# Expert weights prepared while stage A empties, own orders of work for its filling and emptying, and its loop written out

## The reference

```python
x = layernorm(x + attention(x, Wq, Wk, Wv, Wo, bo))   # 16 heads of 8
x = layernorm(x + retention(x, ctx, ctx))             # rotated q and k, decay mask, 16 heads of 8, no weights
x = layernorm(x + moe(x, gate, w1, w3, w2))           # 8 experts, inner 512, top 2 of 8 by gate
# moe: out = sum over the chosen e of p_e * ((silu(x @ w1[e]) * (x @ w3[e])) @ w2[e])
```

## Time and profile before

| what | value |
|---|---|
| median of the runs | 1058.34 us |
| profiled execution, its own time | 1065.84 us |
| its span | 1063.7 us |
| mean granted TensorE clock | 0.903 |
| TensorE busy | 856.2 us, 80% |
| VectorE busy | 800.6 us, 75% |
| GpSimd busy | 650.5 us, 61% |
| ScalarE busy | 621.2 us, 58% |
| stage A, to the first matmul of stage B | 0 to 675.2 us |
| stage B | 675 to about 1003 us |
| stage C | to 1063.7 us |

### The profile page before, as it was taken

One profiled execution on the slowest core, in us unless ns is written; L12 is line 12 of the kernel. 1 busy time (PEld: TensorE's weight loads), 2 busy tenths in 40 slices (PEclk: granted clock), 3 DMA queues, 4 the chain that ended last, 5 costly groups with the idle time before them and its releaser, 6 DMA issues.

```text
span 1063.7 us, 36375 instructions
## 1 busy us (share of the span) xinstructions
PE 856.2 (80%) x12164; PEld 640.8 (60%) x12165; DVE 800.6 (75%) x2219; ACT 621.2 (58%) x1416; POOL 650.5 (61%) x738
## 2 busy tenths in 40 slices
PE   1573969899999899898987871599999999999600
PEld 1352546666567566565655541488888888888600
DVE  3776779999789788797765653588887888777565
ACT  1032446677667666676566862466666666666445
POOL 0353756699989989899777546144444444444443
PEclk9685989999999999999889975799999999999855
DMA  6223211222212313222121101222122112122076
GB/s 231 61 52 83 55 36 39 51 62 53 68 47 62 72 40 71 49 51 61 32 53 50 35 29 61 63 62 57 56 60 59 58 57 58 56 60 57 33 254 220
DMA packets 145252, 72.10 MB, mean 68 GB/s; under 512 B 75024, under 2 KB 134544, under 8 KB 145136
## 3 DMA queue, kind: packets, MB, share of 16 engines
q1 hardware_dynamic: 124800, 40.56, 16.3%
q0 software_dynamic: 8640, 17.84, 5.0%
q10 hardware_dynamic: 11696, 12.08, 3.5%
HBM read 42.11 MB, written 28.34 MB: 66 GB/s over the span
## 4 chain that ended last, share of the span: by engine, by line
PE 36%; POOL 7%; issue 5%; DMA 3%; DVE 3%; ACT 2%; SPq 1%; another core or an unknown queue 0%; POOLq 0%; ACTq 0%; DVEq 0%
PE QKV L770 9%; PE ST L770 9%; PE XT L798 5%; PE SC L798 5%; POOL prod_ev L1550 4%; POOL routed_rows L1567 2%; DMA prod_ev<-token_halves 2%; PE ST L640 1%; ACT q L923 1%; PE YY L788 1%; PE ST L655 1%; PE TR L788 1%; PE YY L588 1%; POOL rs L1530 1%; DMA routed_rows<-xe,pos 1%
## 5 line engine op out<-in xcount | busy, mean ns | idle before, releaser
L1550 POOL TENSOR_TENSOR prod_ev<-e_sb,q_v 128x512 f32<-128x512 f32 x256 | 295.9, 1190 | 101.3 <-PE YY L588 61.6
L1599 POOL DMA_INDIRECT token_halves<-w_new,tok_i x142 | 137.9, 971 | 39.4 <-issue 33.6
L1567 POOL DMA_INDIRECT routed_rows<-xe,pos x128 | 131.4, 1026 | 30.4 <-issue 29.4
L1150 DVE TENSOR_TENSOR prod_qk<-q_v,QKV 128x2048 f32<-128x2048 f32 x64 | 145.4, 2274 | 0.0
L1036 ACT ACTIVATE prod_qk<-QKV,silu_scale 128x512 f32<-128x512 f32 x142 | 95.9, 687 | 61.5 <-PE QKV L770 60.0
L1452 DVE TENSOR_TENSOR prod_ev<-prod_qk,prod_ev 128x1024 f16<-128x1024 f32 x71 | 87.0, 1225 | 54.2 <-ACT prod_ev L1027 34.4
L770 PE MATMUL QKV<-k_t,w_hl 128*128 128x256 f16 x852 | 117.1, 274 | 0.1
L770 PE MATMUL ST<-k_t,w_hl 128*128 128x256 f16 x852 | 117.0, 274 | 0.1
L411 POOL TENSOR_TENSOR marks<-half_c 128x1 f32<-128x1 f32 x103 | 19.9, 193 | 151.1 <-DVE w_new L1468 150.9
L1478 DVE SCALAR_TENSOR_TENSOR prod_qk<-ST,hid_scale,prod_qk 128x512 f32<-128x512 f32 x142 | 102.4, 744 | 10.1 <-ACT prod_qk L1036 7.1
L923 ACT ACTIVATE q<-XT,tab 128x256 f32<-128x256 f32 x256 | 96.6, 497 | 0.0
(11 more groups left out here) (169 smaller groups left out, 1791.9 us busy)
## 6 DMA issues: line engine op xcount, KB each, us to landing
w_new<-routed_rows SPq DMA_DIRECT2D x71, 130.0 KB
prod_ev<-token_halves SPq DMA_DIRECT2D x16, 512.0 KB, 5.0
x_sb<-x SPq DMA_DIRECT2D x32, 128.0 KB, 2.6
x_res<-x SPq DMA_DIRECT2D x128, 32.0 KB
head_rows<-o_n SPq DMA_DIRECT2D x32, 128.0 KB
o_t<-head_rows SPq DMA_DIRECT2D x64, 64.0 KB
ctx_sb<-ctx SPq DMA_DIRECT2D x32, 128.0 KB
out<-prod_qk ACTq DMA_DIRECT2D x16, 256.0 KB, 4.4
```

Source lines behind the costliest of these rows:

```text
L1150: eng.tensor_tensor(prod_qk[:, u, :, :].rearrange("p d (i j) -> p d i j", j=NH), q.unsqueeze(3).to_broadcast([P, HD, NH, NH]), k.unsqueeze ...
L1550: ins = eng.tensor_tensor(prod_ev[:, u, q, :, :, 0:HD], e_sb[:, it.slot(2), u, 64 * q:64 * q + 64].rearrange("p (i j) -> p j i", j=4).unsq ...
L1567: eng.indirect_dma_start(out=xs, out_offset=bass.IndirectOffsetOnAxis(ap=pos[:, r, 2 * u + k:2 * u + k + 1], axis=0), in_=xe[:, r, u, k, : ...
L1599: eng.indirect_dma_start(out=halves, out_offset=bass.IndirectOffsetOnAxis(ap=tok_i[:, s, u:u + 1], axis=0), in_=yw[:, s, u, :], in_offset= ...
```

## The change

1. **Weights.** Their preparation leaves the filling. w1 is loaded ahead of the first step on ScalarE's queue, and stays in `w_new`. Everything else is called in the emptying, at steps named by `last(at, lag)`, the step at which duo 31 has that lag. All three matrices go through `w_new` one after the other: `load_weights(1)` waits until the low part of w1 is done, `load_weights(2)` until that of w3 is. `q8` no longer holds w3. The spread uses QKV in place of ST.
2. **Orders.** `fill`, `step` and `drain` are now separate orders on TensorE, VectorE, ScalarE and GpSimd: `fill` for the first N_FILL = 13 steps, `drain` once the last duo has entered. `step` is in a new order too. In steps 0 to 16, 29 to 31 and in `drain`, `wait_last` waits for every valid pair of its list (`mixed`) and not only for the first.
3. **Loop.** A_FIRST = 32, so no step is left for the loop.
4. **Zero rows.** They lie in `prod_ev` and are set by GpSimd (`blank_pads`) between the two scatters of duo 31.
5. VectorE's lags are all 2 smaller, SyncE's lags for the context and the heads too, which only moves them against SyncE's loads of x.

```diff
-    A_FIRST = 20
-    PE_LAGS, ACT_LAGS, DVE_LAGS, POOL_LAGS, SP_LAGS = 13, 13, 14, 11, 9
-    CTX_LAG, HEADS_LAG = 9, 8
+    A_FIRST = 32
+    PE_LAGS, ACT_LAGS, DVE_LAGS, POOL_LAGS, SP_LAGS = 18, 20, 19, 11, 7
+    CTX_LAG, HEADS_LAG = 7, 6
+    N_FILL = 13
...
             if 0 <= item.off - back < n:
             item.eng.wait_ge(sem, item.off - back + 1)
-            return
+            if not item.mixed:
+                return
...
     for s in range(first):
-        alone(s)
+        alone(s, fill if s < n_fill else body, 0 < n_fill and not n_fill + 4 <= s < n - 3)
...
     for s in range(n, n + lags):
-        alone(s)
+        alone(s, drain or body, drain is not None)
```

ScalarE, ahead of the steps and in the emptying (`high(n)` is the old high part with `w_new` as input):

```diff
+            load_weights(0)
+            eng.wait_ge(blank_ready, 1)
+            eng.dma_start(xs[n_exp * region:n_exp * (region + TILE), :].rearrange("(n p) c -> p n c", p=P),
+                          spare_rows).then_inc(blank_out, 16)
...
+            def drain(at):
+                if last(at, 12):
+                    high(1)
...
+                if it := at(13):
+                    row_ids(it)
+                if last(at, 7):
+                    load_weights(1)
+                if it := at(11):
+                    rows_across(it)
...
+                if it := at(12):
+                    other_over_own(it)
+                if last(at, 12):
+                    load_weights(2)
...
+                if last(at, 20):
+                    high(2)
+                if it := at(9):
+                    ret_across(it)
+                if last(at, 5):
+                    high(0)
+                if it := at(8):
+                    queries_across(it)
```

VectorE in the emptying (`measure`, `weight_scales` and `low` are the old operations, one matrix at a time), and the orders on TensorE and GpSimd there:

```diff
+            def drain(at):
+                if it := at(1):
+                    score_max(it)
+                if last(at, 2):
+                    measure(0)
+                if last(at, 11):
+                    low(1)
+                if last(at, 5):
+                    low(0)
+                if last(at, 4):
+                    weight_scales(0)
...
+                if it := at(8):
+                    mask(it, 0)
+                if it := at(11):
+                    one_hot(it)
+                    chosen(it)
...
+                if it := at(12):
+                    positions(it)
+                if it := at(8):
+                    mask(it, 1)
...
+                if it := at(10):
+                    logits(it)
+                if last(at, 7):
+                    measure(1)
...
+                if last(at, 16):
+                    weight_scales(2)
+                if last(at, 14):
+                    measure(2)
...
+                if last(at, 9):
+                    weight_scales(1)
...
+                if last(at, 19):
+                    low(2)
```

```diff
+                if it := at(10):
+                    ret_values(it)
+                if it := at(9):
+                    queries_across(it)
+                if it := at(11):
+                    rows_across(it)
...
+            def blank_pads():
+
+                for u in range(2):
+                    eng.wait_ge(sums_done[u], n_duo)
+                eng.memset(pad_rows[:, :, 0:P + 1], 0.0)
+                eng.tensor_copy(pad_rows[:, :, P + 1], const("spare_ids")[:, 0:2 * n_exp]).then_inc(blank_ready, 1)
...
+                if it := at(11):
+                    scatter(it, 0)
+                if last(at, 11):
+                    blank_pads()
```

More of the change, by code:

```diff
@@ L90, with __init__ @@
 class Item:
[L93 to L94 removed]
+    def __init__(self, eng, i, snaps, off, mixed=False):
+        self.eng, self.i, self.snaps, self.off, self.mixed = eng, i, snaps, off, mixed
     def slot(self, n):
@@ L426, in wait_norms, with last @@
                 wait(d, sem, back - NORM_GAP)
-        def at_step(at, n):
-            it = at(0)
-            return it is not None and it.i is None and it.off == n
-        MEASURE, SPREAD_AT, HIGH, LOW, FETCH_LAST = (1, 3, 6), (3, 5, 8), (3, 5, 8), (4, 6, 9), 5
-        SPREAD = ST[:, 0:P]
+        def last(at, lag):
+            it = at(lag)
+            return it is not None and it.off == n_duo - 1
+        SPREAD = QKV[:, 0:P]
         def pairs(ap):
@@ L627, in before_ret_scores @@
                 if u == 0:
-                    if it.i is None and it.off == 0:
-                        eng.wait_ge(top_ready, 3)
                     wait(it, q8_ready)
@@ L731, in step @@
                     gates(it)
+                if it := at(7):
+                    residual(it)
+                if it := at(10):
+                    ret_values(it)
                 if it := at(9):
@@ L1004, in step @@
                     residual(it)
-                weights(at)
-            run_steps(eng, n_duo, A_FIRST, ACT_LAGS, step)
+            def step(at):
+                if it := at(9):
+                    blocks(it)
+                if it := at(0):
+                    tokens_across(it)
+                if it := at(4):
+                    beside(it, 0)
+                if it := at(11):
+                    rows_across(it)
+                if it := at(1):
+                    project(it)
+                if it := at(12):
+                    other_over_own(it)
+                if it := at(8):
+                    keys_across(it)
+                if it := at(10):
+                    second_norm(it)
+                if it := at(13):
+                    row_ids(it)
+                if it := at(4):
+                    beside(it, 1)
+                if it := at(8):
+                    first_norm(it)
+                if it := at(2):
+                    exponent(it)
+                if it := at(9):
+                    ret_across(it)
+                if it := at(8):
+                    queries_across(it)
+                if it := at(6):
+                    residual(it)
@@ L1144, in products, with low @@
+            def low(n):
+                eng.wait_ge(hi_ready, n + 1)
+                hl = (w1_hl, w3_hl, w2_hl)[n]
+                eng.scalar_tensor_tensor(out=hl[:, 1, :], in0=w_new[:, :], scalar=w_scale[:, n:n + 1], in1=hl[:, 0, :],
+                                         op0=ALU.mult, op1=ALU.subtract).then_inc(lo_ready, 1)
             def products(it, u):
@@ new lines, in fill, with step @@
+                if it := at(3):
+                    one_over(it)
+                    divide(it)
+                if it := at(11):
+                    gate_weights(it)
+            def step(at):
+                if it := at(12):
+                    positions(it)
+                if it := at(1):
+                    score_max(it)
+                if it := at(6):
+                    spread(it, res1, stat1, res1_ready, stat1_ready, mv1_ready)
+                if it := at(8):
+                    mask(it, 0)
+                if it := at(6):
+                    moments(it, 0, stat1, stat1_ready, mv1_ready)
+                if it := at(11):
+                    one_hot(it)
+                if it := at(1):
+                    max_of_two(it)
+                if it := at(0):
+                    products(it, 0)
+                if it := at(8):
+                    mask(it, 1)
+                if it := at(1):
+                    max_of_four(it)
+                    subtract_max(it)
+                if it := at(7):
@@ new lines, in step @@
+                if it := at(6):
+                    keys_by_cos(it)
+                if it := at(0):
+                    products(it, 1)
+                if it := at(8):
+                    second_residual(it)
+                    spread(it, res2, stat2, res2_ready, stat2_ready, mv2_ready)
+                if it := at(10):
+                    top_values(it)
+                if it := at(3):
+                    one_over(it)
+                if it := at(6):
+                    keys_by_sin(it)
```

488 lines of the change are left out of this document (328 added, 160 removed).

## The result

The changed kernel takes 1093.92 us (median of 4 runs, 1089.74 to 1097.83) against 1058.53 for the kernel before beside it: ratio 1.0316, 95% interval 1.0274 to 1.0359. It is 35 us slower; 24 us faster was forecast. The profiled executions are 1091.4 and 1063.7 us long, so 27.7 us of the loss are in the two traces compared here.

What follows compares the result with a forecast made beforehand. Stage A was taken to have four limits: VectorE in the filling, GpSimd's pace in the even part, a chain of turns in the emptying, then the end. 46 + 14 - 7 - 29 = 24 us gained, 1034 us; range 1018 to 1056.

Steps and rivals of the forecast that it cites:

- The filling: Start to m_own of duo 12: weights' work leaves VectorE, steps of 9.6 us; gain 46 us (36 to 50).
- the deduction for waits: Filling: added waits of mixed cost a little under a quarter of a microsecond a step, lowering 48.3 to 46.
- The loop: Duos 12 to 31: four long intervals at the loop's edges fall to 16.0 us each, saving 11.7 us.
- The even order: Duos 12 to 31: new step order takes 15.9 us against 16.0, gaining 2 us for 19 intervals.
- rival A: Even part: TensorE comes late, steps over 16.0 us; at 17.6 the kernel is 9 us slower, 1067; chance 0.12.
- The order of the operations on the retention's way is hardly changed: Even part: argument given against rival A, that TensorE's lateness would lengthen the steps.
- The emptying: After duo 31 enters: weights' work in the turns, 3.7 + 2 + 3 - 2, loses 7 us (-2 to 20).
- 2 less was forecast: Emptying until GpSimd's last prod_ev: even steps of 15.8 us instead of two longer ones give 2 us back.
- The five turns behind it: Emptying after GpSimd's last prod_ev: turns of 11.0 us, plus 3.7 for high(0), 2 for measure(1), 3 for later q8.
- The end: After duo 31's gates: w3 and w2 chained through w_new, VectorE leaves at 684.5 instead of 655.4; loss 29 us (24 to 36).
- the 19.8 that I left unchanged: End of stage A: silu_scale to stage B's first matmul keeps its 19.8 us, zero rows included.
- the forecast of 36: m_own of duo 31 to stage B's first matmul: emptying's loss of 7 us and the end's of 29.

Runs made afterwards that it cites:

- all_waits: Changed kernel with the added waits of wait_last in every step, the even part too: ratio 1.0335 to the kernel before, step 18.83 us.
- written_out: Kernel before with only A_FIRST raised from 20 to 32, so no loop in stage A: ratio 0.9905 to the kernel before.
- old_pool: Changed kernel with GpSimd's even order alone put back to that of before: ratio 1.0524 to the kernel before, step 19.48 us.
- changed_again: The changed kernel run once more, unaltered, when TensorE's signals came promptly: ratio 1.0321 to the kernel before.
- kick_vectore: written_out with one extra reduce over w_new on VectorE at duo 17, result unused: ratio 0.9982 to the kernel before.
- one_hot_later: Changed kernel with one_hot moved behind logits, directly ahead of chosen, in VectorE's even order: ratio 0.9886 to the kernel before.
- wait_values: Changed kernel with GpSimd waiting for the retention values' signal ahead of a duo's first scatter, duos 3 to 22: ratio 1.0796 to the kernel before.
- one_order: Changed kernel without fill: filling and even part in the order of before, no added waits, drain as changed: ratio 1.001 to the kernel before.

## Why the prediction was wrong

**The filling: right, with parts that cancel.** 45.7 against 46. Duo 0 at 24.3 (25.9 forecast), steps of 9.4, 9.7, 9.1, 8.6 and 8.9, where the prediction says 9.6 "and none shorter"; then 105.0 to duo 12 in place of 98.5. Together duo 12 comes at 175.0, forecast at 172.4 before the deduction for waits. No run shows a cause for that deduction: *all_waits* shows no price of the waits, and with prompt signals the same filling ends at 171.1 to 175.3, without its waits and its order at 170.4.

**The loop: right.** 11.7 forecast, 9.8 between the marks and 10 in the runs of *written_out*. One of the four intervals was no part of it (17.7, still 17.2).

**The even order: the step that failed.** It reads "I take 15.9 against 16.0", since GpSimd needs 15.8 us of work. Summed work is a lower bound of a step, and the new order comes to it with `one_hot` moved: 15.70. But nothing in the sum says that a given order does reach it. As changed it took 18.75, and 17.96 with prompt signals. I gave rival A a price of 17.6 and named TensorE's lateness as its place. Its outcome came, and with prompt signals its place is where the lateness shows: the sums wait for `max_of_two`. Its cause I had not read, a `one_hot` that is held by GpSimd's `prod_ev`. It was visible in the trace of before: `one_hot` there lasts 142 to 1169 ns between 300 and 460 us, for the same 128x16, and the longest is as long as one `prod_ev`:

```profile
L1283 DVE TENSOR_TENSOR oh<-tab,ix x20: 142/234/1169, 304.6 to 453.3; 128x16 f32<-128x16 f32 x20
```

VectorE's old order has `one_hot` ahead of `max_of_two` too. What is new is that GpSimd's scatters went to the start of its step, so that `one_hot` meets a run of up to six `prod_ev` with only `nb` between them. "The order of the operations on the retention's way is hardly changed" was beside the point. The range failed with it, since A was left outside.

That this explains the profiled execution of the changed kernel itself is not shown. There only one of 18 `one_hot` was long (2.9 us), in *all_waits*, with the same step and late signals, nine of 18 (1.2 to 2.9 us). What both traces have in all but two of the 19 even steps is a signal of the retention values that is 2.1 to 2.3 us late, with a scatter that starts some 0.5 us ahead of their end; in the trace of before it comes within 0.05 us. *old_pool* took this away and was slower still. Moving `one_hot` was only run where signals are prompt, so which of the two makes the 35 us of the first measurement stays open; the 3.2% of *changed_again* are `one_hot`.

**The emptying: mis-sized.** 7 forecast, 11.5 measured: the gates of duo 31 end 126.1 us after its m_own, before 114.6. From m_own of duo 31 to the third copy of rt, where GpSimd still holds, it is 45.8 us against 43.4; here 2 less was forecast and 2.4 more came. The five turns behind it (copies of rt at 577.1, 590.6, 605.5, 619.8, 631.3 and 644.7) take 67.6 us against 58.6 before, 9.0 more where the terms of the prediction give 8.7; before they took 11.7 each and not the 11.0 of the one turn that was read. But the terms are not those forecast. The largest turn, 14.9, has the high part of w1 in it, as forecast. The next, 14.3, has no weights' work on its path: ScalarE waits 5.45 us until a scatter has landed, a term that the prediction put at nothing, with the copy of rt behind it:

```profile
591.05 3.71 ACT L917 ACTIVATE w_hl<-w_new,w_scale 128x4096 f16<-128x4096 f32 x1
594.66 3.00 ACT L991 ACTIVATE q<-XT,tab 128x256 f32<-128x256 f32 x8
...
618.21 1.65 ACT L1018 ACTIVATE xe<-res,nb,rs 128x128 f32<-128x128 f32 x4 [5.45 <-DMA routed_rows<-xe,pos]
```

**The end: the chain right, what follows it wrong.** From the gates to silu_scale it is 33.0 us against 4.4, so 29 as forecast. But from silu_scale to the first matmul it is 13.5 us and not the 19.8 that I left unchanged. The difference lies in VectorE's chain of small instructions from silu_scale to the table: 8.5 us after, 15.0 before; from the table to the first matmul it is 5.0 and 4.7. Before, the chain ran beside GpSimd's last scatters, and VectorE's own signals came up to 1.5 us late there, most of them 0.5:

```profile
657.06 0.15 DVE L1396 TENSOR_SCALAR hid_scale<-w_inv 128x1 f32<-128x1 f32 x1 [1.48 <-DVE silu_scale L1395]
```

After, the last scatter had ended 12 us ahead of silu_scale. In *kick_vectore*, with prompt signals, the chain takes 9.1 us beside scatters. So 11.5 + 29 - 6.3 = 34 meets the forecast of 36 because two misses cancel, 4.5 too little in the emptying and 6.3 too much behind silu_scale.

**The whole.** With `one_hot` moved, the mechanism of the forecast runs (ratio 0.9886, 12 us), still half of the 24. A trace of the kernel before with prompt signals is missing. The nearest is *kick_vectore*, which has the old orders without the loop, and one reduce more. Against it the trace of *one_hot_later* gains 47.7 us up to m_own of duo 12 (218.8 to 171.1) and 7.1 over the 19 steps (305.4 to 298.3), and loses 42.4 from duo 31 to stage B (130.0 to 172.4). So by these two traces moving the weights costs 42 us with prompt signals and not 36, since the old end is quicker there (130.0 against 138.7 in the trace of before).

## What to carry to other kernels

Before an instruction order is changed, look for short operations whose duration varies, min against max of one line: here a VectorE operation with two SBUF inputs hid its waiting for GpSimd in busy time. Keep a short one of this kind away from what the other engines wait for, or place it beside GpSimd's DMA issues. The work of the busiest engine is a lower bound of a step, not a forecast of it. Orders written for several engines belong together: here each of the three that were undone alone made the kernel slower. And run the control beside every experiment.

## What the runs showed of the hardware

**A blocked VectorE operation waits for a whole run of GpSimd instructions.** Up to 4.2 us for 128x16 elements over `prod_ev` x2, `nb`, `prod_ev` x2; in *changed_again* and *wait_values* eight of these operations each took 2.4 to 4.2 us between 300 and 460 us. The gaps between GpSimd's instructions did not let it in.

**A scatter of GpSimd can be held by VectorE in turn.** The issue of one scatter took 4.93 us beside the low part of w3 (128x4096, two SBUF inputs), about 1.0 us elsewhere. It is the same in the traces of *changed_again*, *one_hot_later* and *one_order*. `one_hot` beside a scatter took 0.16 us and held nobody.

```profile
661.37 4.93 POOL L1838 DMA_INDIRECT routed_rows<-xe,pos  x1 [0.30 <-issue]
```

**TensorE's signals can come late beside GpSimd's indirect DMAs.** In the trace of the changed kernel the retention values end at 296.05, 0.5 us after the first of two scatters starts; ScalarE's copy, which needs nothing else, starts at 298.29, 0.4 us after the second ends:

```profile
294.97 1.08 PE L648 MATMUL ST<-sm,ctx_bd 128*32 128x128 f32 x32
295.54 1.06 POOL L1838 DMA_INDIRECT routed_rows<-xe,pos  x1 [0.17 <-issue]
296.91 0.96 POOL L1838 DMA_INDIRECT routed_rows<-xe,pos  x1 [0.31 <-issue]
298.29 0.59 ACT L1009 COPY rt<-ST 128x512 f32<-128x512 f32 x1 [3.19 <-remote]
298.93 0.69 PE L659 MATMUL ST<-tab,rt 128*64 128x64 f32 x16 [1.78 <-ACT rt L1009]
```

In that trace groups of matmuls that end 0.5 us after the start of a pair signal some 2.2 us late (median), at 1.5 us 1.25, at 2.5 us 0.4, so all at about one moment. In *changed_again*, the same program, the groups near scatters signalled within 0.13 us from 180 to 530 us. VectorE's, ScalarE's and GpSimd's own signals were within 0.04 us beside the scatters of the even part in both traces; only at the end of stage A, in the trace of before and of *written_out*, do VectorE's come 0.5 to 1.7 us late too. What differs between the two surroundings is not known. The kernel before is about 1.5% slower in the late one.
